# One GNN layer on one Trainium2 core: register loads cut into fours, the residual input moved behind the sums, and more one-hots on ScalarE

## The reference

```python
sums = jax.ops.segment_sum(edge_attr, src, num_segments=n)
counts = jax.ops.segment_sum(jnp.ones((edge_attr.shape[0],), edge_attr.dtype), src, num_segments=n)
edge_attr_agg = sums / jnp.maximum(counts, 1.0)[:, None]
u_expanded = u[batch]                       # batch is all zeros: one row of u
combined = jnp.concatenate([x, edge_attr_agg, u_expanded], axis=1)
h = jax.nn.relu(combined @ W1 + b1)         # 448 -> 512
y = h @ W2 + b2                             # 512 -> 256
out = layernorm(x + y)                      # over the last axis, no scale
```

## Time and profile before

| | value |
|---|---|
| median of three runs | 801.06 us (800.24 to 801.56) |
| profiled execution, span from first to last instruction | 799.5 us |
| around the span (median less span) | 1.5 us |
| granted TensorE clock, mean | 0.994 |
| PE busy | 745.1 us (93%), 11398 matmuls |
| DVE busy | 716.8 us (90%), 2382 |
| ACT busy | 501.7 us (63%), 998 |
| POOL busy | 417.1 us (52%), 410 |
| `sup<-sorted_rows` loads | x129, 396.0 KB each, 4.0 us to landing |

### The profile page before, as it was taken

The page is one execution under the profiler, slowest core; times in us unless marked ns, Lnnn a source line. Parts: engine busy times, 40 slices in busy tenths (PEclk is TensorE's granted clock), DMA queues, the critical chain, the costliest instruction groups (busy, mean ns, idle before and its releaser), DMA issues.

```text
span 799.5 us, 31269 instructions
## 1 busy us (share of the span) xinstructions
PE 745.1 (93%) x11398; PEld 711.5 (89%) x11399; DVE 716.8 (90%) x2382; ACT 501.7 (63%) x998; POOL 417.1 (52%) x410
## 2 busy tenths in 40 slices
PE   8889999999999999999999888989898986899995
PEld 4689999999999999999999888989898986899995
DVE  8999999999999999999896388989898988799995
ACT  1366676666667767667667545555555552688886
POOL 3087777777677787877776400000000002788983
PEclk9999999999999999999999999999999999999999
DMA  6366556666665666656674678999999990012122
GB/s 215 131 210 204 201 202 211 213 215 219 202 219 195 212 220 211 225 205 214 203 210 167 239 227 260 281 282 282 285 283 285 281 277 10 27 52 64 53 66 64
DMA packets 75268, 156.38 MB, mean 196 GB/s; under 512 B 11084, under 2 KB 51277, under 8 KB 75097
## 3 DMA queue, kind: packets, MB, share of 16 engines
q1 hardware_dynamic: 58328, 102.33, 42.5%
q0 software_dynamic: 16896, 53.54, 17.9%
HBM read 95.47 MB, written 60.37 MB: 195 GB/s over the span
## 4 chain that ended last, share of the span: by engine, by line
PE 60%; DVE 30%; issue 5%; ACT 2%; POOL 1%; DMA 1%; DVEq 0%; ACTq 0%; SPq 0%; POOLq 0%
PE ps L858 33%; DVE onehot L1236 18%; PE ps L785 11%; PE ps L936 5%; PE ps L990 3%; DVE pre L1275 2%; DVE perm L1146 2%; DVE stats L1301 1%; DVE weights_z L1296 1%; PE ps L776 1%; PE ps L792 1%; POOL h_low L628 1%; PE ps L811 1%; PE ps L843 1%; PE ps L841 1%
## 5 line engine op out<-in xcount | busy, mean ns | idle before, releaser
L600 POOL DMA_INDIRECT sorted_rows<-payload,idx x264 | 304.8, 1155 | 131.8 <-issue 51.9
L858 PE MATMUL ps<-attr_buf,perm 128*128 128x198 bf16 x3168 | 302.6, 252 | 1.1 <-ACT attr_buf L642 0.8
L858 PEld LDWEIGHTS ps<-attr_buf,perm 128*128 128x128 bf16 x3168 | 288.6, 96 | 6.1 <-ACT attr_buf L642 1.2
L649 ACT CAST payload<-ps 128x792 bf16<-128x792 f32 x264 | 217.9, 825 | 76.7 <-PE ps L858 62.2
L1146 DVE TENSOR_SCALAR perm<-place_of,pos 128x512 bf16<-128x512 int16 x792 | 241.1, 362 | 3.4 <-PE ps L858 2.7
L1236 DVE TENSOR_SCALAR onehot<-node_of,sup 128x256 bf16<-128x256 int16 x903 | 192.4, 284 | 41.9 <-PE ps L936 22.3
L936 PE MATMUL ps<-sup,onehot 128*128 128x64 bf16 (+1 forms) x6192 | 196.1, 193 | 24.7 <-DVE onehot L1236 21.0
L936 PEld LDWEIGHTS ps<-sup,onehot 128*128 128x128 bf16 x6192 | 193.5, 98 | 27.3 <-issue 27.3
L619 POOL TENSOR_TENSOR xs<-xs,b_all 125x256 f32<-125x256 f32 x50 | 37.6, 775 | 209.4 <-DMA xs<-in_x 209.4
L713 ACT ACTIVATE apart<-node_of,sup 128x256 bf16<-128x256 int16 x129 | 65.6, 508 | 94.3 <-PE ps L936 90.2
L785 PE MATMUL ps<-xt,w1x 128*128 128x125 f32 x800 | 99.9, 278 | 5.9 <-DVE pos L1067 3.3
(11 more groups left out here) (150 smaller groups left out, 603.7 us busy)
## 6 DMA issues: line engine op xcount, KB each, us to landing
sup<-sorted_rows SPq DMA_DIRECT2D x129, 396.0 KB, 4.0
attr_buf<-in_edge_attr SPq DMA_DIRECT2D x43, 576.0 KB
out<-weights_z SPq DMA_DIRECT2D x25, 224.0 KB
xs<-in_x SPq DMA_DIRECT2D x12, 448.0 KB
x_stage<-in_x SPq DMA_DIRECT2D x47, 112.0 KB
sorted_rows<-payload,idx POOLq DMA_INDIRECT x264
pre<-jump_d SPq DMA_DIRECT2D x1, 1560.0 KB, 10.4
pre<-first_d SPq DMA_DIRECT2D x1, 780.0 KB, 7.2
```

Of the source, the lines that this page charges most:

```text
L600: pool.indirect_dma_start(out=sorted_rows, out_offset=bass.IndirectOffsetOnAxis(ap=idx[:, n:n + 1], axis=0), in_=payload[s][:, :], in_offs ...
L649: nc.scalar.copy(payload[s][:, :].rearrange("p (r w) -> p r w", w=PART), slots_p[s % PSUM_BUFS]).then_inc(s_pay, 1)
L858: last = nc.tensor.matmul(slot_p[s % PSUM_BUFS][r].rearrange("p (h f) -> p h f", f=PLANE), places, parts(a, t * CB + s), start=(t == 0 and ...
```

## The change

There are three edits, all in the sum stage.

- TensorE's places come four at a time (`find_tables`). The first four are loaded ahead of the loop; then, in supers 2, 6, 10 and 14 of a turn, after the six matmuls of slot 0, the four places of the next group of supers are loaded. `where_row` becomes the first tensor in SBUF.
- The residual input is loaded behind the last super, in five pieces of 10 columns with a semaphore each. GpSimd waits for a piece when it first needs it. SyncE's turns become one loop.
- ScalarE makes slot 3 of three supers in four (k = 0, 1, 2 of 4), not of two. VectorE makes 3, 3, 3, 4 one-hots for four supers, where it made 3, 4, 3, 4.

```diff
@@ constants
+PLACES_AT_ONCE = 4
+ACT_OF = 4
+ACT_TURN = BODY // ACT_OF * (ACT_OF - 1)
+def act_slots(k):
+    return k // ACT_OF * (ACT_OF - 1) + min(k % ACT_OF, ACT_OF - 1)
-X_TURN = 3
-X_COLS = 4
+X_COLS = 10
@@ SBUF: where_row now ahead of ident
+        where_row = sb("where_row", [1, 2 * SUPER_COLS * P], I32)
         ident = sb("ident", [P, P])
@@ SyncE
             super_turn(0, found=True)
-            for m in range(1, X_TURN):
+            with sp.Fori(1, SUP_TURNS) as m:
                 super_turn(m)
+            super_turn(SUP_TURNS, SUPER_PAIRS - SUP_TURNS * PAIR_BUFS)
             sp.wait_ge(s_pre, COLS + 1)
-            with sp.Fori(X_TURN, X_TURN + X_PIECES) as m:
-                super_turn(m)
+            for k in range(X_PIECES):
                 for lo, hi in ((0, XPART), (XPART, NP)):
-                    sp.dma_start(xs[lo:hi, bass.ds(m * X_PIECE - X_TURN * X_PIECE, X_PIECE)],
-                                 x_v[lo:hi, bass.ds(m * X_PIECE - X_TURN * X_PIECE, X_PIECE)]).then_inc(s_xs, 16)
+                    sp.dma_start(xs[lo:hi, k * X_PIECE:(k + 1) * X_PIECE], x_v[lo:hi, k * X_PIECE:(k + 1) * X_PIECE]
+                                 ).then_inc(s_xs[k], 16)
@@ GpSimd
-            pool.wait_ge(s_xs, 2 * 16 * (X_PIECES + 1))
             def add_b2(g):
+                if g % (X_COLS // 2) == 0:
+                    pool.wait_ge(s_xs[g // (X_COLS // 2)], 2 * 16)
@@ ScalarE super_turn
-                for k in range(0, count, 2):
-                    act.wait_ge(s_sup[k // 2], m * 16 + 16)
+                for k in range(count):
+                    if k % ACT_OF == ACT_OF - 1:
+                        continue
+                    n = act_slots(k)
+                    if k % 2 == 0:
+                        act.wait_ge(s_sup[k // 2], m * 16 + 16)
@@ TensorE
+            def find_tables(k, at):
+                pe.load(table_regs[k:k + PLACES_AT_ONCE], where_row[0:1, bass.ds(at, PLACES_AT_ONCE)])
             def super_turn(m, count=BODY):
-                pe.load(table_regs[0:count], where_row[0:1, bass.ds(m * BODY, count)])
                 for k in range(count):
-                    if k % 2 == 0:
-                        pe.wait_ge(s_hot_a, m * PAIR_BUFS + (k // 2 + 1))
+                    if k % ACT_OF != ACT_OF - 1:
+                        pe.wait_ge(s_hot_a, m * ACT_TURN + act_slots(k + 1))
                     for r in range(SLOTS):
...
+                        if r == 0 and k % PLACES_AT_ONCE == 2 and count == BODY:
+                            following = k - 2 + PLACES_AT_ONCE
+                            find_tables(following % BODY, m * BODY + following)
                     last.then_inc(s_added, 1)
+            find_tables(0, 0)
             with pe.Fori(0, SUP_TURNS) as m:
@@ VectorE super_turn
-                    for r in range(SLOTS - 1 + k % 2):
+                    for r in range(SLOTS if k % ACT_OF == ACT_OF - 1 else ACT_SLOT):
```

More of the change, by code:

```diff
@@ L97 @@
 SUP_TURNS = SUPER_PAIRS // PAIR_BUFS
+PLACES_AT_ONCE = 4
+assert 2 * SUPER_PAIRS - SUP_TURNS * BODY <= PLACES_AT_ONCE
 ACT_SLOT = SLOTS - 1
+ACT_OF = 4
+ACT_TURN = BODY // ACT_OF * (ACT_OF - 1)
+def act_slots(k):
+    return k // ACT_OF * (ACT_OF - 1) + min(k % ACT_OF, ACT_OF - 1)
 TURN = 3
@@ L114 @@
 Z_BUFS = 3
-assert X_TURN + X_PIECES + 1 == SUP_TURNS
+assert X_PIECES * X_COLS == COLS and X_COLS % 2 == 0 and X_COLS // 2 >= B2_AHEAD
 STEPS = COLS // 2
@@ L151, in build @@
         eps_col = sb("eps_col", [P, 1])
-        where_row = sb("where_row", [1, 2 * SUPER_COLS * P], I32)
         node_of = sb("node_of", [P, 2 * P], I16)
@@ L366, in build @@
         s_table = sem("s_table")
-        s_xs = sem("s_xs")
+        s_xs = [sem(f"s_xs{k}") for k in range(X_PIECES)]
         s_xb = sem("s_xb")
@@ L709, in super_turn @@
             def super_turn(m, count=BODY):
-                for k in range(0, count, 2):
-                    act.wait_ge(s_sup[k // 2], m * 16 + 16)
+                for k in range(count):
[4 more added lines that the diff above has]
+                        act.wait_ge(s_sup[k // 2], m * 16 + 16)
                     act.wait_ge(s_added, m * BODY + (k + 1 + SUP_FREE - HOT_BUFS))
-                    nc.scalar.activation(apart[k // 2 % 2][:, :], node_of[:, :], ACT.Abs, scale=-1.0,
+                    nc.scalar.activation(apart[n % 2][:, :], node_of[:, :], ACT.Abs, scale=-1.0,
                                          bias=place_in[k][:, ACT_SLOT, :]).then_inc(s_apart, 1)
-                    act.wait_ge(s_apart, m * PAIR_BUFS + (k // 2 + 1))
-                    nc.scalar.activation(onehot[k % HOT_BUFS][:, ACT_SLOT, :], apart[k // 2 % 2][:, :], ACT.Relu, scale=-1.0,
+                    act.wait_ge(s_apart, m * ACT_TURN + (n + 1))
+                    nc.scalar.activation(onehot[k % HOT_BUFS][:, ACT_SLOT, :], apart[n % 2][:, :], ACT.Relu, scale=-1.0,
                                          bias=1.0).then_inc(s_hot_a, 1)
```

## The result

The changed kernel takes 793.93 us, the median of four runs (792.51 to 794.39), against 801.31 us for the kernel before on the same chip: 0.9905 of it, 95% interval 0.989 to 0.992. It is 7.4 us faster; 808.2 was forecast, slower by 7. The profiled execution spans 791.9 us, the one before 799.5. The stage after the sums lasts the same in both (127.9 and 128.0 us behind the last matmul's start), so the gain lies in the sum stage, which went from 219.0 to 211.4 us.

A forecast was written before the change was run, and what follows sets the result against it. The prediction took PE to bound each turn, with load gaps between turns. Its terms, +28.8 load idles, +3.0 turn ends, -1.5 first turn, -23.2 removed gaps, gave +7.1 us: 808.2 us, range 781 to 816 (forecast's own 803 to 814).

The forecast's parts named there:

- the price of a load of four: TensorE's load of four places in the sum stage: taken as 0.55 us, with 0.51 and 0.70 as ends.
- A load under 0.45 us: Sign on TensorE's loads of four places: a duration under 0.45 us would show the forecast wrong; 0.51 to 0.60 was expected.
- C: Rival on TensorE's loads: paid by the register or slowed, 0.70 us, idle 0.60 a load, 818 us; chance 0.08.
- PE is the bound inside a turn, and 23.2 us hang on the places: Sum stage: PE never idles within turns; removing 15 gaps of 1.5 us and one of 0.7 saves 23.2 us.
- The sequencer stands still during the load: TensorE, mid-super loads: nothing behind the load is issued meanwhile, so the array has only queued matmuls, 0.70 us of cover.
- Rival A: TensorE's loads don't hold the matmuls behind them: all 64 idles go, 781 to 789 us; chance 0.27.
- Idle of 0.45 for each load: PE behind each mid-super load: 1.16 us of sequencer work less 0.70 of cover, idle 0.45; 64 loads add 28.8 us.
- A turn's end without a load, 0.2 us: PE at the loop's end, no load there: 0.2 us idle with the restart; 15 of them add 3.0 us.
- The first turn swallows 1.5 us: First turn of the sum stage: PE waits for the first pairs anyway, which hides 1.5 us of its four load idles.
- ScalarE and VectorE: nothing: One-hots in the sum stage: ScalarE's extra share fits and VectorE's saving is hidden by the matmuls; 0 us.
- The residual input: nothing in the turns; GpSimd's additions at 0, with an end of -1.5: Moved input: no gain in turns, late load hidden; GpSimd's b2 additions still slow VectorE's one-hots, 0, ends -1.5 and +1.5 us.
- Rival B: TensorE's loads covered a little better: idle of 0.25 to 0.38 us a load, 796 to 804 us; chance 0.10.

## Why the prediction was wrong

The failed step is one term: "I take 0.55, the nearest on the same engine", the price of a load of four. It is 0.332. The ends that I kept, 0.51 and 0.70, didn't hold it either. A load under 0.45 us was also the first sign that the prediction named for being wrong. I had drawn a line through loads of 1, 2, 8 and 16 registers, and there is no such line. One of the rows was also read wrongly: SyncE's 0.507 for one register stands right behind the issue of the last piece of the residual input, just as the 0.70 for eight does. Where that piece is gone one register takes 0.284, so eight cost SyncE 0.24 more than one, not 0.03, as was said against C. The first row is of the kernel before, ahead of its load at 655.8, the second of the changed one:

```profile
654.84 0.93 SPq L531 DMA_DIRECT2D xs<-in_x  x2
...
L512 SPq TENSOR_LOAD <-where_row x1: 284/284/284, 650.5 to 650.5; - x1
```

What the runs show fits a price by fetches: TensorE needs 0.332 for four registers, 0.593 for eight, 1.11 for sixteen, so one fetch of four and then 0.26 for each further four (0.332 + 3 x 0.26 = 1.11). Where four can't be fetched together, because there are only two or because they begin 4 bytes off such a step of 16, each seems to cost by itself: 0.538 for two, 1.00 for four. On SyncE one register took 0.284 and eight 0.523, and shifted, 1.67. The row of 0.556 that I leaned on was a load of two: it was true, and it was of the other kind. That the price is a matter of single and fourfold fetches is my reading of eight durations and isn't shown otherwise; that four registers take 0.33 us from a multiple of 16 bytes in the row and 1.00 from 4 bytes behind one is measured.

With the measured price the rest of the sum stands but for small terms, step by step:

- *PE is the bound inside a turn, and 23.2 us hang on the places.* Right. The gaps at the turns' heads and the last one sum to 22.2 us in the starts of the matmuls, and the kernel without loads in its loop, which keeps the turns' ends (2.0 us in its trace) and has lost the wait beside GpSimd (1.5), lies 21.5 us under the kernel before, against 22.2 - 2.0 + 1.5 = 21.7.
- *The sequencer stands still during the load; Rival A.* The forecast's mechanism is right and A is wrong: a gap of 0.21 us or more comes at 63 of the 64 places (0.02 at the other, in the first turn), and its size obeys load + 0.056 - queued x 0.0305, where 0.056 is the time from the load's end to the next matmul, the same within 0.002 at all 58 places from super 18 to 246. With 5 queued: 0.332 gives 0.235 (measured 0.234), 0.593 gives 0.496 (0.487), 1.002 gives 0.905 (0.907). With 10 queued 0.083 (0.075). With 13 queued -0.01 (none). The section Sequencer Loop of the Trainium skill's page Advanced Engine Details and Errata, by which other engine instructions can be read and queued during a control instruction, isn't borne out by this trace for a register load.
- *Idle of 0.45 for each load.* 0.235, all of the difference from the load's duration (0.55 - 0.33 = 0.22). The five register operations and the cover were sized right.
- *A turn's end without a load, 0.2 us.* 0.148.
- *The first turn swallows 1.5 us.* Its gaps of over 0.05 us sum to 2.87 us, against 2.49 before, so by these two traces it swallowed 0.6 of its four idles' 0.94 us and not 1.5. The term isn't settled: with the same four loads in the first turn, the other runs' traces have 2.0 to 4.5 us there.
- *ScalarE and VectorE: nothing.* Right, by the run with ScalarE at two of four and by the one without loads. The slack was larger than reckoned: where ScalarE doesn't wait, its pair repeats each 0.86 us, not 0.96.
- *The residual input: nothing in the turns; GpSimd's additions at 0, with an end of -1.5.* The end came: I put the additions 5 us later but still beside one-hots; they began at 664.4, VectorE's last one-hots ended at 661.7, 8 us sooner than before (669.5). So this term hung on the first: the stage was faster, where the forecast had it slower. In the two runs of the moved input whose stage is slower than before, with loads of two and with shifted places, the additions still meet one-hots, which take 0.77 us. 1.5 us of gaps from super 246 on went.

The sum with these: 64 x 0.235 = 15.0, less 0.6 for the first turn, + 15 x 0.148 = 2.2, - 22.2, - 1.5 = -7.1 us; measured -7.4 in the medians and -7.6 in the span. Rival B lay nearest: a load cheaper than reckoned, with an idle of 0.25 to 0.38 and 796 to 804 us; the measured 0.235 and 793.9 lie just below both. It had a chance of 0.10. The rule of the Trainium skill weighed in C (Runtime: NRT & Kernel Launch, section Instruction fetch mechanics: about 200 ns for each register) is given on a page that describes such loads as coming from HBM, where these come from SBUF. It misses the load of four, 0.8 against 0.332, by more than my row did; in the run with shifted places, 1.67 / 8 = 0.21 on SyncE and 1.00 / 4 = 0.25 on TensorE are near it.

## What to carry to other kernels

Ask of a short sequencer operation how much work is queued on the engine when it starts, not how much was issued before it: moving the load from behind 6 matmuls to behind 18 was worth 12 us, more than the whole change. Put it where the queue is full and where a matmul, not another register operation, follows. And do not draw a line through durations of different sizes: two registers cost more than four, so the price of the size that you need wants its own run; where a term has 64 copies, an error of 0.2 us decides the sign.

No run moved the load into a super without cutting it up (that would need a second set of 16 registers). By the relation above, one load of 16 behind six matmuls would leave a gap of 1.11 + 0.056 - 5 x 0.0305 = 1.01 us, 1.16 a turn with the turn's end. This is an estimate. The four loads of the changed kernel leave 4 x 0.235 + 0.148 = 1.09, two loads of eight 2 x 0.49 + 0.145 = 1.12, and the load at the head left 1.43. So most of the gain seems to come from the new place, away from the branch, and little from the cut into fours.

## What the hardware showed that I hadn't expected

- A load of 2 registers took 0.538 us, of 4 0.332, of 8 0.593, of 16 1.11 on TensorE; a load of 4 that begins 4 bytes off a multiple of 16 in the row 1.00. The first load of the stage takes about 0.19 more in every run (0.524 in the changed kernel).
- SyncE's load of 8 took 0.523 us, and 0.69 to 0.71 where it stands right behind the issues of a piece of the residual input; its load of 1 took 0.284 and 0.50 to 0.52. So it is in all four runs with that input in the turns. The issue of a pair of supers (396 KB) just as close ahead leaves it at 0.523.
- VectorE's one-hot of 0.28 us takes about 0.76 beside GpSimd's additions, in each of the six traces in which they meet; in the other eight no one-hot of this stage takes over 0.3.
- About 17 matmuls are issued ahead of the array; when a load starts behind 6, 12, 18 or 24 matmuls of a super, mostly 4 or 5, 9 or 10, 13 and 13 are left, since register operations of 0.1 us each come in between.
